# Transposes moved from TensorE to DMA, scales to GpSimd and a bias folded, in a decoder layer's kernel

## The reference

```python
q, k, v = (split(x @ W.T + b) for W, b in ((Wq, bq), (Wk, bk), (Wv, bv)))      # 16 heads of 16
q_phi, k_phi = apply_kernel(q, orf), apply_kernel(k, orf)     # exp(proj - norm), 64 features a head
out = einsum(q_phi, einsum(k_phi, v)) / einsum(q_phi, sum(k_phi))
x = layernorm(x + out @ Wo.T + bo)
kh, qh, vh = ctx @ Wk.T, x @ Wq.T, ctx @ Wv.T                 # per head, 16 x 16
x = layernorm(x + softmax(qh @ kh.T / 4) @ vh)
# act_quant(x) = clip(round(x * s), -128, 127) / s with s = 127 / max|x| of the row; weights ternary
h = silu(act_quant(x) @ ternary(w_gate).T) * (act_quant(x) @ ternary(w_up).T)
x = layernorm(x + act_quant(h) @ ternary(w_down).T)
```

## Time and profile before

| | us |
|---|---|
| median of 3 runs | 506.53 (505.39 to 511.43) |
| profiled execution | 505.92 |
| its span, first to last instruction | 504.2 |
| PE busy in the span | 438.9 |
| VectorE (DVE) busy | 450.6 |
| ScalarE (ACT) busy | 428.8 |
| GpSimd (POOL) busy | 365.5 |

### The profile page before, as it was taken

How to read it: one execution, slowest core, us unless ns; L and a number is a source line. 1 busy time by engine, 2 the same in 40 slices (tenths; PEclk the granted TensorE clock), 3 DMA queues, 4 the chain that set the end, 5 groups by cost and what they waited for, 6 DMA issues and landing times.

```text
span 504.2 us, 18524 instructions
## 1 busy us (share of the span) xinstructions
PE 438.9 (87%) x6566; PEld 304.7 (60%) x6566; DVE 450.6 (89%) x1355; ACT 428.8 (85%) x908; POOL 365.5 (72%) x789
## 2 busy tenths in 40 slices
PE   4568888998999998999999999999999999876641
PEld 2235666666776766776767676777676766543310
DVE  4667686999999999899999999999999999999771
ACT  2247789999999998999999999999999999867532
POOL 1447767778788888788888888888888876763422
PEclk9979899999999999999999999999999999999875
DMA  7665566787768787566666666666666687542212
GB/s 186 230 125 101 133 116 109 107 154 124 127 130 134 157 140 133 133 146 146 146 146 141 140 139 135 144 140 142 136 145 136 137 139 127 85 75 62 55 33 63
DMA packets 192659, 64.27 MB, mean 127 GB/s; under 512 B 172384, under 2 KB 192352, under 8 KB 192608
## 3 DMA queue, kind: packets, MB, share of 16 engines
q1 hardware_dynamic: 190080, 60.46, 60.4%
q10 hardware_dynamic: 2528, 3.15, 1.7%
HBM read 17.31 MB, written 4.19 MB: 43 GB/s over the span
## 4 chain that ended last, share of the span: by engine, by line
PE 58%; ACT 13%; DMA 11%; DVE 7%; issue 5%; SPq 3%; POOL 3%; ACTq 0%; POOLq 0%; DVEq 0%
PE bank L1131 10%; PE bank L1335 9%; DMA tT<-pkT 4%; PE bank L1306 4%; PE bank L1225 4%; PE bank L1362 4%; PE bank L1183 3%; DMA ffn_ld<-in_L_ffn_w_down_dram 3%; PE bank L1204 2%; PE bank L1145 2%; PE bank L1240 2%; PE bank L1322 2%; PE bank L1150 2%; PE bank L1211 2%; PE bank L1294 2%
## 5 line engine op out<-in xcount | busy, mean ns | idle before, releaser
L1131 PE MATMUL bank<-wq_hi,xT 128*128 128x512 f16 (+1 forms) x256 | 72.5, 338 | 3.7 <-DVE vv L816 2.3
L434 POOL TENSOR_TENSOR ve<-mv,lneps 128x1 f32<-128x1 f32 x96 | 19.4, 202 | 63.4 <-DVE mv L866 48.0
L438 POOL TENSOR_TENSOR rs<-ve,mhalf 128x1 f32<-128x1 f32 x96 | 55.0, 573 | 0.0
L946 DVE SCALAR_TENSOR_TENSOR g<-th,bank 128x512 f32<-128x512 f32 x64 | 43.4, 678 | 4.7 <-ACT th L653 4.3
L558 ACT ACTIVATE x<-y,nmr,rs 128x256 f32<-128x256 f32 x64 | 39.8, 622 | 7.9 <-DVE y L1007 4.4
L630 ACT ACTIVATE pT<-bank 128x512 f32<-128x512 f32 x64 | 37.8, 591 | 9.7 <-PE bank L1296 8.1
L897 DVE TENSOR_REDUCE negm<-bank 128x4 f16<-128x512 f32 x64 | 43.4, 678 | 1.6 <-PE bank L1260 1.2
L898 DVE TENSOR_REDUCE negm<-bank 128x4 f16<-128x512 f32 x64 | 43.5, 680 | 0.0
L577 ACT ACTIVATE phk<-bank 128x512 f32<-128x512 f32 x64 | 39.4, 617 | 4.5 <-PE bank L1150 4.5
L1131 PE MATMUL bank<-wq_lo,xT 128*128 128x256 f16 (+1 forms) x128 | 43.2, 337 | 0.0
L425 POOL TENSOR_TENSOR pkA<-qk,pkA 128x512 f16<-128x512 f32 x32 | 37.6, 1175 | 7.0 <-ACT pkA L520 6.6
(11 more groups left out here) (184 smaller groups left out, 1580.0 us busy)
## 6 DMA issues: line engine op xcount, KB each, us to landing
xs<-in_x_dram SPq DMA_DIRECT2D x32, 128.0 KB, 2.3
cs<-in_ctx_dram SPq DMA_DIRECT2D x32, 128.0 KB, 2.3
xr<-in_x_dram SPq DMA_DIRECT2D x32, 128.0 KB, 2.3
out_dram<-ot SPq DMA_DIRECT2D x32, 128.0 KB, 1.8
ffn_ld<-in_L_ffn_w_gate_dram ACTq DMA_DIRECT2D x1, 1024.0 KB, 9.0
ffn_ld<-in_L_ffn_w_up_dram ACTq DMA_DIRECT2D x1, 1024.0 KB, 11.5
ffn_ld<-in_L_ffn_w_down_dram ACTq DMA_DIRECT2D x1, 1024.0 KB, 13.8
pkAT<-pkA SPq DMA_TRANSPOSE x64, 3.2
```

Of the source, the lines that this page charges most:

```text
L438: g.tensor_tensor(rs[n - 1][:, :], ve[n - 1][:, :], mhalf[:, :], ALU.pow).then_inc(done[f"pw{n}"], 1)
L946: v.scalar_tensor_tensor(g1[:, n, :], th[:, n, :], 1.0, gate, ALU.add, ALU.mult).then_inc(done[f"gl{n}"], 1)
L1131: last = T.matmul(o, xT[:, 2 * part + c, :], w[:, c, cols], start=(n == 0), stop=(n == 5))
```

## The change

- The two transpose DMAs for queries (`qT`) and keys (`kT`) become one of 2048 columns, which waits for what `kT` waited for.
- x and xq are transposed by DMAs on the SP queue (`xT_`, 512 columns of fp16, and `xqT_`, 256 columns of bf16) into double buffers; the TensorE steps `xTp`, `xqTp` and ScalarE's copies go.
- The value bias is multiplied by Wo once, before the loop (`value_bias`), and added to the output bias (`output_bias`); the values leave PSUM on ScalarE as a scaled copy (`v_`), not on VectorE.
- `sg` and `sd` move from VectorE to GpSimd.
- The maxima stand in 16 columns in place of 128 (negm, nmT), and one DMA writes both rows.
- The order of every engine's list, the lags, the PSUM banks and the waits that protect them are made anew; `load_down` is issued after `evacuate_wo`; the reductions and roundings of the feed-forward weights start in other passes, and GpSimd no longer waits for the output bias ahead of its list.

```diff
@@ SP @@
+            def xT_(t, par):
+                wait_ahead(sp, t, par, ("xlo", 0))
+                transpose(xT[:, par, :, :], xpk[:, :, :].rearrange("p n d -> p (n d)"), "xT", par)
+
+            def xqT_(t, par):
+                wait_ahead(sp, t, par, ("xqf", 0))
+                transpose(xqT[:, par, :, :], xq[:, par, :], "xqT", par)
             def qT(t, par):
-                wait_ahead(sp, t, par, ("phq0", -1))
-                transpose(pkAT[:, 0:PAIRS, :], pkA[:, 0:PAIRS, :, :].rearrange("p c r d -> p (c r d)"), "qT", par)
-
-            def kT(t, par):
-                wait_ahead(sp, t, par, ("lo", 0), ("nlo", 0), ("phk0", -1))
-                transpose(pkAT[:, PAIRS:H, :], pkA[:, PAIRS:H, :, :].rearrange("p c r d -> p (c r d)"), "kT", par)
+                wait_ahead(sp, t, par, ("lo", 0), ("nlo", 0), ("phq0", -1))
+                transpose(pkAT[:, :, :], pkA[:, :, :, :].rearrange("p c r d -> p (c r d)"), "qT", par)
             def row(t, par):
                 wait(sp, "mT", t)
-                for p in (32, 96):
-                    sp.dma_start(tT[p:p + 1, par, :, :], nmT[p:p + PAIRS, :]).then_inc(moved["row"][par], 16)
+                sp.dma_start(tT[32:P:64, par, :, :], nmT[:, :]).then_inc(moved["row"][par], 16)
             def iteration(i, par):
+                go(tT_, i, par, 7)
+                go(load_x, i, par, 0)
+                go(store, i, par, 13)
+                go(load_r, i, par, 3)
+                go(cT_, i, par, 6)
+                go(xqT_, i, par, 9)
                 go(load_c, i, par, 4)
-                go(load_r, i, par, 4)
-                go(load_x, i, par, 0)
-                go(kT, i, par, 3)
                 go(hqT_, i, par, 10)
-                go(store, i, par, 13)
+                go(xT_, i, par, 1)
                 go(row, i, par, 7)
                 go(qT, i, par, 3)
-                go(tT_, i, par, 6)
-                go(cT_, i, par, 5)
@@ GpSimd: its new list is sd nf rs2 xb_ clo xlo rs1 xqf lo hq0 hq1 sg ya2 chi phe rs3 xhi @@
+            def sg(t, par):
+                first_time(pool, t, 0, scales, 5)
+                g.tensor_tensor(sgate[:, par:par + 1], acl[:, :], cgate[:, :], ALU.mult)
+                g.tensor_scalar(sprod[:, par:par + 1], acl[:, :], cprod[:, :], acl[:, :], ALU.mult,
+                                ALU.mult).then_inc(done["sg"], 1)
+
+            def sd(t, par):
+                g.tensor_tensor(sdown[:, par:par + 1], hcl[:, :], cdown[:, :], ALU.mult).then_inc(done["sd"], 1)
@@ ScalarE: its new list is th0 v_ x1T_ th1 aT sq thi vh kvm_ ot_ p1 p0 x2_ nT_ hi oxT_ hm0 hm1 ephk1 ephk0 ephq1 ephq0 x1_ mT @@
-            def xT_(t, par):
-                wait(act, "xTp", t)
-                copy(xT[:, :, :], at_xT.bitcast(F16).rearrange("p (c t) -> p c t", c=4), "xT")
+            def v_(t, par):
+                first_time(act, t, 0, prep, 14)
+                wait(act, "vm", t)
+                copy(vv[:, par, :, 0:DK], at_v.rearrange("p (h d) -> p h d", h=H), "v", 1.0 / WSCALE)
@@ VectorE: its new list is ad1 bs1 hx y1 am ac hc ar hr qnt hs nr m0 nhi rx nlo oxn m1 bs3 rd qk_ vsm at y3 bs2 kve y2 gl0 gl1 hu0 tlo hu1 ad3 hh1 hh0 @@
+            def output_bias():
+                dve.wait_ge(prep_ps, 6)
+                dve.wait_ge(bo_in, 16)
+                v.tensor_tensor(bob[:, :], at_bias, bo_ld[:, :], ALU.add).then_inc(rep, 1)
@@ TensorE @@
+            def value_bias():
+                pe.wait_ge(prep_ev, 4)
+                pe.wait_ge(rep, 7)
+                for k in range(2):
+                    last = T.matmul(at_bias, bv_rep[:, k, :], woT[:, k, :], start=(k == 0), stop=(k == 1))
+                last.then_inc(prep_ps, 1)
             def iteration(i, par):
+                go(u0, i, par, 8)
+                go(aTp, i, par, 4)
+                go(vhp, i, par, 6)
+                go(tm, i, par, 5)
+                go(kvp, i, par, 3)
+                go(u1, i, par, 8)
+                go(dn, i, par, 9)
+                go(st1, i, par, 6)
+                go(st0, i, par, 6)
+                go(wo, i, par, 4)
+                go(nump, i, par, 3)
+                go(pv1, i, par, 6)
+                go(pv0, i, par, 6)
+                go(s0, i, par, 5)
+                go(s1, i, par, 5)
+                go(qkm, i, par, 0)
+                go(phk1, i, par, 2)
+                go(oxp, i, par, 6)
+                go(phk0, i, par, 2)
+                go(phq1, i, par, 2)
+                go(ntp, i, par, 3)
+                go(phq0, i, par, 2)
+                go(kvs, i, par, 2)
+                go(g0, i, par, 7)
+                go(mTp, i, par, 5)
+                go(vm, i, par, 0)
+                go(g1_, i, par, 7)
+                go(x1Tp, i, par, 4)
```

More of the change, by code:

```diff
@@ L644, in oxT_ @@
                 copy(oxT[:, :, :], at_pv.rearrange("p (c t) -> p c t", c=4), "oxT")
-            def xqT_(t, par):
-                wait(act, "xqTp", t)
-                copy(xqT[:, :, :], at_xq.bitcast(BF16).rearrange("p (c t) -> p c t", c=2), "xqT")
             def th0(t, par):
@@ L704, in _ @@
+                once(evacuate[4], i, 5)
+                go(mT, i, par, 4)
             run(act, iteration)
@@ L1323, in oxp, with inner @@
                 last.then_inc(done["oxp"], 1)
-            def xqTp(t, par):
-                wait(pe, "xqf", t)
-                wait(pe, "vh", t, 2)
-                dst = at_xq.bitcast(BF16)
+            def inner(o, w, n, par, name):
                 for k in range(2):
-                    last = T.transpose(dst[:, k * P:(k + 1) * P], xq[:, par, k * P:(k + 1) * P], idb[:, :])
-                last.then_inc(done["xqTp"], 1)
-            def inner(o, w, n, name):
-                for k in range(2):
-                    last = T.matmul(o, xqT[:, k, :], w[:, k, 512 * n:512 * n + 512], start=(k == 0), stop=(k == 1))
+                    last = T.matmul(o, xqT[:, par, k, :], w[:, k, 512 * n:512 * n + 512], start=(k == 0), stop=(k == 1))
                 last.then_inc(done[name], 1)
```

427 lines of the change are left out of this document (191 added, 236 removed), and 10 rows, old and new, of the table done.

## The result

The changed kernel takes 520.47 us, the median of four runs (516.25 to 524.46), beside 506.62 us (505.39 to 511.43) of the kernel before on the same chip. Run once more it gave 520.15 us (six runs, 514.61 to 523.97). Runs more than 1.5% above the fastest of their kernel are left out of the ratios and of all comparisons from here on, and then the changed kernel takes 517.6 and 517.8 us, ratios 1.0215 (95% interval 1.0119 to 1.0311) and 1.0217 [1.0161, 1.0273]. The forecast was 492 us; either way the measured time lies outside its range of 482 to 508.

The account below looks back on a forecast made before the run. PE, DVE and ACT were taken to be full at once in the middle, with latency at both ends. From 505.9 us, -13.0 for 26 tiles, 0 at the start and -0.6 at the end gave 492.3, stated as 492, range 482 to 508.

Parts of the forecast that it names:

- The largest holds: 12.6: Middle: a tile takes the largest of DVE 12.27, ACT 12.52, PE 12.67 and the loop through tT, 12.61 us.
- PE's term of -0.35 us: PE, per tile: the transposes of x and xq go, 0.24 and 0.11 us on the chain.
- The other terms: Other engines, per tile: DVE -0.75 us, ACT net -0.50 us, POOL about 0.6 us more within its idle time.
- x 26: Middle: 0.50 us gained per tile against the mean of 13.10, times 26 tiles, -13.0 us.
- the second rival: The gain is eaten: new PE waits on xqT at g0 and tT at s0, 0.35 to 0.5 us a tile; 505 us; chance 0.24.
- The third rival: tT's transfer lands late, behind the joined transpose: with a landing of 4.3 us, +12 us, 518 us; chance 0.12.
- The cover of 0.14 us: From tm to the next s0: PE's own work 5.27 us over tT's path of 5.13, cover 0.14 instead of 0.68 us.
- Its order matters more than its sum: SP queue: a little fuller in a shorter tile but not full, transposes 7.2 to 7.5 us a tile against 6.25 before.
- my two assumptions: Transpose issue on SP: by size (2.5 us joined, 0.6 for x, 0.3 for xq) or a fixed price of 1.25 us each.
- The start, put at 0: Start: +2.6 us for the first x's landing against DVE's 2.68 us wait for w_down; 0, bounds -5 and +6.
- The end, put at -0.6: End: -3.0 us from DVE and +2.4 for the last xq; -0.6 us, bounds -5 and +4.
- The 3.0 us that DVE should have given back: End: eight tiles with 0.75 us less on DVE, half of it on the chain, -3.0 us.

Follow-up runs that it names:

- after_again: The changed kernel itself run once more, nothing changed, with more rounds: median 520.15 us of six runs (514.61 to 523.97).
- x_none: The changed kernel with x's transpose left out from tile 2 on, a plain 4 KB copy in its place (output not the reference's): 516.19 us, ratio 1.0166.
- unjoin2: The changed kernel with the joined transpose of queries and keys taken apart, both halves at its place, keys first: 524.57 us, ratio 1.0374.
- x_first: The changed kernel with the loads of x for tiles 0 and 1 issued ahead of the weights: 511.4 us, ratio 1.009.
- unjoin: The changed kernel with the joined transpose taken apart, the keys' half at its place, the queries' half directly behind tT's: 551.06 us, ratio 1.0865.
- xf_xq: The changed kernel with x's loads for tiles 0 and 1 ahead of the weights and xq transposed on TensorE: 512.64 us, ratio 1.0102.
- xf_xq14: The changed kernel with x's first two loads ahead of the weights, xq transposed on TensorE, and 14 instead of 16 written-out passes: 512.35 us, ratio 1.0063.
- xq_pe: The changed kernel with xq transposed by two TensorE instructions and a ScalarE copy again, not by a DMA: 514.1 us, ratio 1.0118.

## Why the prediction was wrong, point by point

**The bound of the middle: right mechanism, 0.2 us wrong.** "The largest holds: 12.6" was rounded down from PE's own 12.67, and PE's term of -0.35 us was probably too large. PE's busy time went from 141.66 / 11 = 12.88 to 139.31 / 11 = 12.66 us, -0.21, and with the waits that it keeps, 0.14 us, a tile takes 12.81. (The split isn't firm: after_again has the same 140.9 us with 137.46 us of PE, in a trace with ten fewer of its records.) I had taken PE's saving from durations of the chain and the old tile length from DVE's full row; the length that PE alone would have needed (12.88 + 0.13 = 13.01) stood in the same row. The other terms hold: DVE 142.69 - 137.78 = 4.91 us in 11 tiles, -0.45 busy (its starts are closer than its durations), POOL +0.53. ACT went down by 0.38 rather than 0.50.

**"x 26": the step that failed.** I multiplied one tile's gain by 26 tiles, though only the last 11 or 12 run in an even way. For the 15 before I had forecast -7.5 us, and +3.8 was measured. I had read the landing of tT, 3.1/3.3/5.3, as one number. By stage it is two. tT's landings before, in the written-out stretch and in the loop (min/median/max):

```profile
DMA to landing us min/median/max: 3.2/3.3/5.3
DMA to landing us min/median/max: 3.3/3.3/3.3
```

and after:

```profile
DMA to landing us min/median/max: 3.1/3.3/5.2
DMA to landing us min/median/max: 3.1/3.3/3.4
```

So tT lands no later than before, in neither stretch. What is gone is the cover. Before, a landing of 3.3 us is there 0.68 us ahead of s0 (318.81 + 3.3 = 322.11; s0 at 322.79); after, s0 starts within 0.1 us of it (337.91 + 3.1 = 341.0; s0 at 341.10). What that costs where a landing is late is seen in PE's waits for it from tile 5 to 20. Before, after, and x_none (us, times, longest):

```profile
PE bank L1259 <- DMA tT<-pkT: 3.1, 6, 1.4
```

```profile
PE bank L1258 <- issue: 9.4, 7, 2.0
```

```profile
PE bank L1261 <- issue: 7.3, 6, 2.1
```

The 6.3 us more, less the 15 x 0.2 = 3.0 us of PE's own saving, are the +3.8 us of this stretch to within 0.5. That step of the sum, a gain of 0.5 us in each of these 15 tiles, failed because a landing delayed by code, which the kernel before still covered for the most part, is waited for in full. PE also waits for xqT at `g0` there, 1.4 us in three tiles: the second rival's mechanism, and small. The third rival had the right mechanism (s0 waits for tT) and nearly the right total (518), but for the wrong reason: it asked for a landing of 4.3 us in every tile, while the landings are 3.8 to 5.2 us in six tiles of the 15 and 3.1 to 3.3 in the rest, and 9.3 of the 23.9 us of error lie at the two ends. That its total came out near is luck.

**The cover of 0.14 us.** It was worked out with tT issued 1.83 us behind tm. After, it is 337.91 - 335.51 = 2.40 us in one tile and 2.13 in the next (tm at 322.69, tT at 324.82), since tT stands in the queue directly behind a transpose whose issue takes 1.96 us and not 1.26; hqT's, xT's and the row's issue stand right ahead of that. "Its order matters more than its sum" was said of SP, but I didn't add the queue's order into the data path. In the even stretch this costs nothing that can be measured (x_none: same 12.81 us with 0.67 us less on the queue), but it leaves no room: in unjoin2, where two issues of together 2.64 us stand ahead of tT, a tile is 0.22 us longer. In the written-out passes a late landing is paid in full. That PE's own work between tm and s0 shrinks from 5.81 to 5.27 us was right to 0.1 (5.37 in x_none, where nothing waits there); the other part of the lost cover is this later issue.

**The price of a transpose's issue.** Neither of my two assumptions. By size, from the SP queue: 1.17 us for 256 columns, 1.22 for 512, 1.26 to 1.29 for 1024 and 1.96 for 2048. My 2.5 us for the joined one was too much, my 0.3 and 0.6 us for xq and x too little. Their landings in the loop, in the median: 2.3, 2.5, 3.3 and 4.4 us. (In the changed kernel's loop tT's own issue takes 1.28 and 1.55 us by turns.) With them SP is busy for 10.52 us a tile after and 9.11 before.

**The start, put at 0: +2.5.** Its +2.6 us for the first x's transpose were taken from a landing in the middle (3.3 us). Beside the weight loads it was 7.98 us, and tile 0 starts 7.2 us later (22.95 instead of 15.8). Of that 2.5 us are left at tile 5; x_first shows that most of the 4.7 between was slack. Range right, mechanism right, term mis-sized.

**The end, put at -0.6: +6.2.** I had counted xq's landing once, "for the last xq", and as 2.4 us. The chain takes it four times, 2.35 us each, because in the end each of the last tiles is latency. Four times 2.35 less four times the old path's 1.33 - 0.42 = 0.9 us is 5.8 us. That this is close to the 6.2 measured shows nothing: the run that gives xq back to PE recovered only 3.5 of them, the lower granted clock (0.83 instead of 0.89) makes an estimated 6 us of its own, and other parts of the chain got shorter. Shown are the 3.5 us; the other 2.7 stay open. The 3.0 us that DVE should have given back aren't there: no engine is full in this stage, so an engine's saving there counts only where the chain passes it. The rule that I quoted from the Trainium skill, page "VectorE: DVE Perf Modes", section "Rules for kernel authors" (TensorE where PSUM will do), was borne out at both ends of the program. The price for the DMA path in its section "The three transpose paths", 1309 ns, is under what a transfer that is waited for took here: 2.35 us for the two 128x128 blocks of xq at the end, 7.98 us for the four of x at the start.

**Right.** In the loop nothing waits at `g0`, the joined transpose lands in time for `hi`, POOL has room for the scales (128.34 of 140.90 us), and no link of the chain is the value bias.

**Open.** Why the same data take 16% more of the DMA engines' time in written-out passes with only 17 more packets, why some landings with an instruction packet beside them are in time, and what the clock costs at the end. An order of the SP queue with tT ahead of the joined transpose wasn't tried either; in unjoin `hi` stood 1.1 us a tile for a transpose that came later.

## What to carry to other kernels

Cut a profile into its stages before multiplying a tile's gain: code that is written out, a loop and a drain each have their own bound. A shorter engine row was worth nothing here where a landing with a tail of 2 us is just covered, so take the cover from the queue's order and the landing's worst row, not from its median. The transposes moved from TensorE to DMA were free only in the loop, where enough other work covers them. To keep them on TensorE for the first and last tiles alone is the edit that these runs suggest; it was not tried. And compare the granted clock of a drain before you put its whole length down to one wait.

## What the hardware showed that I had not expected

- Written-out passes cost time even where no engine waits for code: eight more of them cost 9.0 us in one kernel and 3.8 in the other, with 17 more instruction packets among 53,000 in the first. In sixteen profiles all 105 late landings of tT had such a packet beside them, and none of the 262 without one was late.
- A transpose DMA's issue costs nearly the same from 256 to 1024 columns (1.17 to 1.29 us), and 1.96 us at 2048: joining two saves 0.6 us of the queue.
- Behind the weight loads a transpose of 512 columns lands after 7.9 to 8.0 us, three times its 2.5 us, whether it is issued at 5.8 or at 15 us (6.6 and 7.3 us in xf_xq and xf_xq14).
- The granted clock of TensorE in the last stage is lower where the stage is longer in three profiles (before, xq_pe, after): 0.89, 0.86 and 0.83 in 102.7, 105.4 and 108.9 us. Eight products that take 0.87 us at the full clock take 1.90 at the lower one.
